# A two-layer decoder block: the shared expert's sums are copied apart and turned a unit later; the narrow attention's first head norms are formed batch by batch

## The reference

```
def _L0_ffn_ref(...):                       # 16 experts, 4 picked per row
    probs = softmax(h @ router_w.T); top_vals, top_idx = top_k(probs, 4)
    y = einsum('eni,eih->enh', silu(g) * u, w_down)
    routed = einsum('enh,ne->nh', y, comb)
    shared = silu(h @ sh_gate) * (h @ sh_up) @ sh_down     # width 704
    return routed + sigmoid(h @ sh_gate_w) * shared

def _L1_attn_ref(...):                      # 16 heads of 16 channels
    q = (_rms(x, g_q) @ Wq + bq); k, v = split(_rms(x, g_kv) @ Wkv + bkv)
    scores = einsum('bhqd,bhkd->bhqk', _rms(q, g_head), _rms(k, g_head)) * 16 ** -0.5
    return (softmax(scores) @ v) @ Wo + bo

x = x + _L0_attn_ref(_layernorm(x), ...)
x = x + _L0_xattn_ref(..., _layernorm(x), ctx)     # time mixing, a scan over the rows
x = x + _L0_ffn_ref(_layernorm(x), ...)
x = x + _L1_attn_ref(_layernorm(x), ...)
x = x + _L1_xattn_ref(_layernorm(x), ctx, ...)
x = x + _L1_ffn_ref(_layernorm(x), ...)
```

## Time and profile before

| | |
|---|---|
| median of 3 runs | 1784.8 us |
| the profiled execution | 1775.09 us, its span 1773.3 us |
| TensorE busy | 1588.2 us, 90% of the span, mean granted clock 0.957 |
| its weight loads | 1281.9 us, 72% |
| DVE / ACT / POOL busy | 1116.2 us, 63% / 946.6 us, 53% / 554.5 us, 31% |
| shared expert's group ends | transposes start at 666.1, 705.3, 740.5 and 763.5 us |
| narrow attention | first scores at 1046.4 us |

### The profile page before, as it was taken

The page is one execution under the profiler, slowest core; times in us unless marked ns, Lnnn a source line. Parts: engine busy times, 40 slices in busy tenths (PEclk is TensorE's granted clock), DMA queues, the critical chain, the costliest instruction groups (busy, mean ns, idle before and its releaser), DMA issues.

```text
span 1773.3 us, 26005 instructions
## 1 busy us (share of the span) xinstructions
PE 1588.2 (90%) x8599; PEld 1281.9 (72%) x8599; DVE 1116.2 (63%) x2497; ACT 946.6 (53%) x2996; POOL 554.5 (31%) x466
## 2 busy tenths in 40 slices
PE   6999999989998768899999769999979999999766
PEld 5888878877877556667777647777758888888534
DVE  3543675677477675454444465655467888877878
ACT  4666655556655643223323435676835565566556
POOL 2233332563254362311001554556131132211000
PEclk9999999999999988999999968989989999999988
DMA  7143234433444062133433411100031111000001
GB/s 268 31 165 127 95 121 140 153 125 105 151 156 151 30 166 66 60 103 124 129 106 115 145 46 31 43 4 25 1 140 30 33 42 34 12 1 1 1 1 48
DMA packets 85241, 147.33 MB, mean 83 GB/s; under 512 B 9700, under 2 KB 45172, under 8 KB 85108
## 3 DMA queue, kind: packets, MB, share of 16 engines
q1 hardware_dynamic: 78964, 128.89, 22.3%
q0 software_dynamic: 6144, 16.79, 3.0%
HBM read 86.65 MB, written 58.98 MB: 82 GB/s over the span
## 4 chain that ended last, share of the span: by engine, by line
PE 46%; DVE 9%; issue 3%; ACT 3%; POOL 2%; another core or an unknown queue 1%; DMA 0%; DVEq 0%; POOLq 0%; ACTq 0%
PE bank L1144 5%; PE bank L906 5%; PE bank L611 4%; PE bank L613 4%; PE bank L612 4%; PE bank L923 4%; PE bank L1135 3%; PE bank L1118 3%; PE bank L1023 2%; PE bank L1005 2%; PE bank L1107 1%; PE bank L1126 1%; PE bank L1012 1%; PE bank L897 1%; PE bank L914 1%
## 5 line engine op out<-in xcount | busy, mean ns | idle before, releaser
L2632 ACT ACTIVATE cross_attention_heads<-cross_attention_heads,small 128x128 f32<-128x128 f32 x256 | 99.6, 390 | 117.2 <-DVE small L2042 117.2
L806 PE MATMUL bank<-self_attention 128*128 128x256 f32 x512 | 125.6, 389 | 22.3 <-ACT self_attention L2376 18.9
L1144 PE MATMUL bank<-cross_attention,cross_attention_heads 128*128 128x256 f32 x512 | 122.1, 381 | 12.7 <-DVE residual L2056 8.2
L2737 POOL CAST qkv_weights_split<-self_attention 128x1024 fp32r<-128x1024 f32 x45 | 50.4, 1119 | 252.6 <-DMA self_attention<-in_wqkv 206.5
L806 PEld LDWEIGHTS bank<-self_attention 128*128 128x128 f32 x512 | 97.7, 194 | 41.2 <-issue 21.7
L2360 ACT ACTIVATE self_attention<-self_attention,small 128x128 f32<-128x128 f32 x256 | 100.2, 394 | 47.0 <-DVE small L1687 45.6
L611 PE MATMUL bank<-x_channel_major,qkv_weights_split 128*128 128x512 f32 x256 | 117.8, 460 | 6.5 <-DVE qkv_weights_split L1720 2.9
L2545 ACT ACTIVATE narrow_late<-bank,small 128x128 f32<-128x128 f32 x256 | 91.2, 376 | 51.4 <-DVE small L1913 50.9
L1144 PEld LDWEIGHTS bank<-cross_attention,cross_attention_heads 128*128 128x128 f32 x512 | 96.1, 190 | 31.2 <-DVE residual L2056 15.1
L2739 POOL TENSOR_TENSOR qkv_weights_split<-self_attention,qkv_weights_split 128x1024 fp32r<-128x1024 f32 x45 | 110.6, 2458 | 3.7
L906 PE MATMUL bank<-experts,tiles 128*128 x316 | 107.6, 463 | 0.2 <-DVE tiles L1792 0.2
(11 more groups left out here) (406 smaller groups left out, 4626.9 us busy)
## 6 DMA issues: line engine op xcount, KB each, us to landing
picked_inputs<-self_attention SPq DMA_DIRECT2D x64, 512.0 KB, 6.5
self_attention<-in_wqkv SPq DMA_DIRECT2D x48, 512.0 KB, 6.0
experts_far<-picked_inputs SPq DMA_DIRECT2D x79, 128.0 KB, 2.1
picked_outputs<-tiles SPq DMA_DIRECT2D x79, 128.0 KB, 1.7
self_attention<-in_wo SPq DMA_DIRECT2D x16, 512.0 KB
experts<-in_moe SPq DMA_DIRECT2D x4, 1408.0 KB
context_values<-context_out SPq DMA_DIRECT2D x16, 256.0 KB
cross_attention<-context_values SPq DMA_DIRECT2D x4, 1024.0 KB, 9.0
```

The costliest lines, as they stand in the source:

```text
L806: m = T.matmul(bank[7][:, 0:D], ZT_a[n % 2][:, h, :], wo_a[p % 2][:, h, :], start=h == 0, stop=h == HG - 1)
L1144: m = T.matmul(bank[7][:, 0:D], ZT_x[n % 2][:, h, :], x_wo[hg % 2][:, h, :], start=h == 0, stop=h == HG - 1)
L2632: m = S.activation(P_x[u][:, h, :], P_x[u][:, h, :], ACT.Exp, bias=negmax_x[u][:, h:h + 1], accum_out=sums_x[u][:, h:h + 1])
```

## The change

*Shared expert.* ACT copies the sums into tiles of their own, e_sum, which lie in the columns of raw4, the raw weights of the narrow attention. So that the place is free, the load of these weights (768 KB) moves in SP's program to expert tile 8. `copy_sums` stands ahead of the cast of the unit in hand, where `finish` stood behind it. TensorE turns the sums in two lots of four transposes (`turn_sum`), each behind one of the next two projections, both into bank 7; for the last group, into banks 6 and 7. DVE adds them in two lots, in the next two steps. The down projection that opens a group now waits for the copies (e_copied), and the expert tiles wait for the last adds only at their down projections.

*Narrow attention.* Logarithm, exponential and inverse root of the first group are formed batch by batch, on 32 columns each. POOL's head norm 0 comes ahead of the square of batch 3, and both gathers ahead of all squares. Only head 0 is transposed before the loop. The scores wait for one half of the spread keys where they waited for both. Two combines move between the keys, the third behind the first scores.

```diff
+HEADS = {0: 1, 1: 2, 2: 3, **{n + 13 + b: GB * g + b for g, n in FIRST_STEPS for b in range(GB)}}
+HEAD_NORMS = [0] + [GB + g for g in range(NG)]
...
-        raw4 = columns(kept, "narrow_attention_weights", KT * 3 * D).take(KT * 3 * D).rearrange("p (k c) -> p k c", k=KT)
+        raw4_all = columns(kept, "narrow_attention_weights", KT * 3 * D).take(KT * 3 * D)
+        raw4 = raw4_all.rearrange("p (k c) -> p k c", k=KT)
+        e_sum = [raw4_all[:, d * GT:(d + 1) * GT] for d in range(KT)]
...
+        def sum_bank(sums, d):
+            return bank[6 + d if sums == NG - 1 else 7]
...
                     if first:
-                        pe.wait_ge(e_added, KT * (sums - 1) + d + 1)
+                        pe.wait_ge(e_copied, KT * (sums - 1) + d + 1)
                     m = matmul3(bank[d][:, :], hi[:, d * P:(d + 1) * P], lo[:, d * P:(d + 1) * P], h_hi, h_lo, first, last)
                 m.then_inc(e_down, 1)
-                if last:
-                    for d in range(KT):
-                        pe.wait_ge(e_copied, KT * sums + d + 1)
-                        for b in range(GB):
-                            m = T.transpose(bank[d][:, b * P:(b + 1) * P], e_gate[d][:, b * P:(b + 1) * P], ident[:, :])
-                        m.then_inc(e_turned, 1)
+            def turn_sum(sums, d):
+                pe.wait_ge(e_copied, KT * sums + d + 1)
+                pe.wait_ge(a_added, NSTEP)
+                pe.wait_ge(e_added, KT * sums)
+                if sums < NG - 1:
+                    pe.wait_ge(e_added, KT * sums + d)
+                for b in range(GB):
+                    m = T.transpose(sum_bank(sums, d)[:, b * P:(b + 1) * P], e_sum[d][:, b * P:(b + 1) * P], ident[:, :])
+                m.then_inc(e_turned, 1)
...
                 if i < NUNIT:
                     up(i)
                 side.step()
+                if unturned:
+                    turn_sum(*unturned.pop(0))
                 if i >= LAG:
                     down(i - LAG)
+                    if UNITS[i - LAG][3]:
+                        unturned += [((i - LAG) // NSH, d) for d in range(KT)]
                 side.step()
             side.finish()
+            for sums, d in unturned:
+                turn_sum(sums, d)
...
                 pe.wait_ge(t_outs, n - 1)
+                pe.wait_ge(e_added, KT * NG)
                 pe.wait_ge(got_down, 16 * len(down_pieces()))
...
             pe.wait_ge(tables_set, 1)
-            pe.wait_ge(e_added, KT * NG)
...
                 pe.wait_ge(n_exp, n - 1)
-                pe.wait_ge(n_spread, bb + 1)
                 i, half = divmod(q4, 2)
+                pe.wait_ge(n_spread, 2 * bb + i + 1)
...
             for b in range(GB):
                 narrow_project(b)
-            for b in range(2):
-                narrow_heads(b)
+            narrow_heads(0)
...
+                if unadded:
+                    add_sum(*unadded.pop(0))
                 if i >= LAG and UNITS[i - LAG][3]:
-                    finish(i - LAG)
+                    unadded += [((i - LAG) // NSH, d) for d in range(KT)]
                 side.step()
             side.finish()
+            for sums, d in unadded:
+                add_sum(sums, d)
...
+            def first_inverse(b):
+                mine, sums = slice(b * 32, (b + 1) * 32), qss[:, 0, b, :]
+                dve.wait_ge(n_root, 2 * b + 2)
+                newton(sums, n_w[:, mine], sums, n_t[:, mine], DS, RMS_EPS).then_inc(n_inverse, 1)
...
+            combine(5)
             split_xt(NORM["second", 0], 1)
             keys_of(15)
+            combine(6)
             for b in range(GB):
                 narrow_project(b)
-                if b:
+                if b >= 1:
                     narrow_sums(b - 1)
+                if b >= 2:
+                    first_inverse(b - 2)
             narrow_sums(GB - 1)
-            combine(5)
-            narrow_inverse(0)
-            combine(6)
-            combine(7)
+            first_inverse(GB - 2)
+            first_inverse(GB - 1)
             for n in range(B * 4 + 6):
                 if n >= 6 and (n - 6) % 4 == 0 and n < B * 4 + 3:
                     narrow_values((n - 6) // 4)
                 if n < B * 4:
                     narrow_scores(n)
+                if n == 0:
+                    combine(7)
                 if n in COMBINE:
...
                 side.step()
-            gate_busy = [(a_scores, NSTEP)] * 2
-            def up(n):
+            def gate(n):
                 u = n % 2
                 act.wait_ge(e_up, 2 * n + 1)
-                act.wait_ge(*gate_busy[u])
+                act.wait_ge(a_scores, NSTEP)
+                act.wait_ge(e_gated, n - 1)
                 S.activation(e_gate[u], bank[2 + u][:, :], ACT.Silu).then_inc(e_silu, 1)
-                gate_busy[u] = (e_gated, n + 1)
+            def split_hidden(n):
+                u = n % 2
                 act.wait_ge(e_gated, n + 1)
                 act.wait_ge(e_down, n - 1)
                 act.wait_ge(a_output, NSTEP)
                 S.copy(e_split[u][0], e_hid[u]).then_inc(e_h_hi, 1)
-            def finish(n):
-                sums = n // NSH
+            def copy_sums(sums):
+                act.wait_ge(fill_done, 12 * NHG * NG)
                 for d in range(KT):
-                    act.wait_ge(e_down, n + 1)
-                    act.wait_ge(*gate_busy[d])
-                    S.copy(e_gate[d], bank[d][:, :]).then_inc(e_copied, 1)
-                    gate_busy[d] = (e_turned, KT * sums + d + 1)
+                    act.wait_ge(e_down, NSH * (sums + 1))
+                    act.wait_ge(e_turned, KT * (sums - 1) + d + 1)
+                    S.copy(e_sum[d], bank[d][:, :]).then_inc(e_copied, 1)
             side.finish()
             side.add(last_group())
             for i in range(NUNIT + LAG):
                 if i < NUNIT:
-                    up(i)
+                    gate(i)
+                if i >= LAG and UNITS[i - LAG][3]:
+                    copy_sums((i - LAG) // NSH)
+                if i < NUNIT:
+                    split_hidden(i)
                 if i in (1, 2):
                     split_weights(i + 3)
-                side.step()
-                if i >= LAG and UNITS[i - LAG][3]:
-                    finish(i - LAG)
-                side.step()
+                side.step(2)
...
                 act.wait_ge(t_up, n + 1)
                 act.wait_ge(t_gated, n - 1)
-                act.wait_ge(e_turned, KT * NG)
+                act.wait_ge(e_gated, NUNIT)
...
             def key_root():
                 act.wait_ge(c_squared, B)
-                act.wait_ge(n_inverse, 1)
+                act.wait_ge(n_inverse, GB)
...
+            def first_root(b):
+                w = n_w[:, b * 32:(b + 1) * 32]
+                act.wait_ge(n_summed, b + 1)
+                S.activation(w, qss[:, 0, b, :], ACT.Ln, bias=eps_rms[:, 0:1], scale=1.0 / DS).then_inc(n_root, 1)
+                act.wait_ge(n_root, 2 * b + 1)
+                S.activation(w, w, ACT.Exp, bias=log_rms[:, 0:1], scale=-0.5).then_inc(n_root, 1)
...
-            narrow_root(0)
-            for b in range(2):
-                narrow_heads(b)
+            for b in range(GB - 1):
+                first_root(b)
+            narrow_heads(0)
+            first_root(GB - 1)
...
             def head_norm(bb):
                 g, b = divmod(bb, GB)
-                pool.wait_ge(n_inverse, g + 1)
+                pool.wait_ge(n_inverse, HEAD_NORMS[g] + 1 if g else b + 1)
...
                 pool.wait_ge(n_heads, bb + 1)
                 pool.wait_ge(n_scores, 4 * (bb - 1))
                 for i in range(2):
-                    m = G.tensor_tensor(kbd[s][:, i], n_kT[bb % 8][:, i].unsqueeze(1).broadcast_to([P, HG, P]),
-                                        mask4.unsqueeze(2).broadcast_to([P, HG, P]), ALU.mult)
-                m.then_inc(n_spread, 1)
+                    G.tensor_tensor(kbd[s][:, i], n_kT[bb % 8][:, i].unsqueeze(1).broadcast_to([P, HG, P]),
+                                    mask4.unsqueeze(2).broadcast_to([P, HG, P]), ALU.mult).then_inc(n_spread, 1)
...
             inverse_deviations(NORM["second", 0], RMS_EPS * LN_EPS, 1.0 + RMS_EPS)
-            for b in range(GB):
+            gather(7)
+            gather(8)
+            for b in range(GB - 1):
                 square(b)
-            gather(7)
             head_norm(0)
-            head_norm(1)
+            square(GB - 1)
             spread_keys(0)
-            head_norm(2)
-            head_norm(3)
-            gather(8)
+            for b in range(1, GB):
+                head_norm(b)
...
                     sp.wait_ge(fill_done, 12 * NHG * NG)
-                    D_(raw4, io["wqkv1"]).then_inc(got_w4, 16)
                     fetch_value(6)
...
                 if n == 8:
+                    D_(raw4, io["wqkv1"]).then_inc(got_w4, 16)
...
```

35 lines of the change are left out of this document (17 added, 18 removed).

## The result

The kernel after takes 1770.57 us (median of 15 runs, 1763.85 to 1784.59), the kernel before 1786.64 us beside it (15 runs, 1779.33 to 1791.78). The ratio is 0.9914, with a 95% interval from 0.9899 to 0.9929: 15.4 us less, between 12.7 and 18.0. Forecast were 19.7 us less and 1765.1 us, with a range of 1758 to 1774. So the time lies in the range, and outside the 1760 to 1769 that the forecast gave for itself; the saving of 19.7 lies outside the measured interval.

What follows compares the result with a forecast made beforehand. TensorE, busy for 90% of the span, was taken as the bound, with time to gain only from its idle tenth or lower clock. Shared expert 8.7 plus narrow start 11.0 made 19.7 us: 1784.8 to 1765.1 us, range 1758 to 1774.

Steps and rivals of the forecast that it cites:

- Rival A: Shared expert gives 4 us or less, as DVE's chain and nameless delays keep it; total 15, 1770 us; chance 0.15.
- First group: Shared expert, first group's sums: DVE sets the stretch, so only 0.5 us gained, ends 0 and 1.6.
- Second: Shared expert, second group's sums: picks no longer stand behind DVE's adds; 0.8 us gained, ends -0.5 and 1.2.
- Third: Shared expert, third group's sums: 6 us gained, taken between 8.1 without the nameless delays and 3.5 to 4.2 with them.
- Its other case: Third group of the shared expert: nameless delays come again at the same instructions, leaving a gain of 3.5 to 4.2 us.
- Last: Shared expert's last group: first tile's transposes need no adds; 1.4 of 2.63 us come back, ends 0 and 2.6.
- Narrow start: Start of the narrow attention: earlier gathers, norms and scores bring score block 3 11.0 us forward, bounds 5 and 12.
- combine(7): DVE's combine behind the narrow attention's first scores, beside three norms: 2 to 4.3 us by the rows, taken as 3.
- Its signs: Shared expert and narrow start: trace marks, including tiles 6 to 11 us earlier; wrong if narrow start gives under 8.
- Rival B: Narrow start gives half: a nameless delay of 5 to 6 us beside the moved gathers; 1771 us; chance 0.14.
- Rival C: Tiles or narrow attention: later waits take back the gain; within 0.2% of 1784.8 us; chance 0.07.
- Rival D: Slower: DMA bursts delay DVE and ACT, 10 us at two points, 3 to 5 in third group; 1790; chance 0.04.

Runs made afterwards that it cites:

- undisturbed pair: The later traces of the unchanged kernels before (e9) and after (e10), without waits that have no named releaser; the two kernels took 1772.2 and 1756.0 us.
- e3: The kernel after with ACT's copies of the sums behind the cast of the unit in hand, as in the kernel before; ratio to before 0.9897.
- e11: The kernel after with ACT's copies behind the cast and POOL's inverse deviations of the narrow attention ahead of gather 6; ratio to before 0.9890.
- first pair: The first traces of the unchanged kernels before and after; the profiled execution of after took 1771.54 us, 3.6 us less than that of before.
- e1: The kernel before with the shared expert's part of the change alone; ratio to before 0.9949, 9.1 us less.
- e4: The kernel after with combines 5 and 6 back behind the first group's inverse roots; ratio to before 0.9905.
- e5: The kernel after with POOL waiting for the last group's last down projection after eight of that group's sixteen scatters; ratio to before 0.9897.
- e12: The kernel of e6 once more, unchanged; ratio to before 0.9918.
- e9: The kernel before, unchanged, timed and traced once more; ratio to before 0.999.
- e10: The kernel after, unchanged, timed and traced once more; ratio to before 0.990.
- e2: The kernel before with the narrow attention's part of the change alone; ratio to before 0.9945, 9.8 us less.
- e7: The kernel after with the gathers of batches 7 and 8 back in their old places behind the squares and head norms; ratio to before 0.9939.
- e8: The kernel after with the first group's roots formed for all four batches at once and head norms behind the fourth square; ratio to before 0.9888.
- e6: The kernel of e5 with POOL also waiting for 5, 9 and 13 keys before gathers 2, 4 and 6; ratio to before 0.9936.

## Why the prediction was right, and where not

The sum was 19.7 us; the undisturbed pair shows 17.1 and the medians 15.4. Faster was forecast, and the time is in the range, which is in part luck: the largest term of the shared expert was four times too large, two smaller ones and the narrow start were too small, and the range was wide enough for Rival A. By its steps:

*First group: forecast 0.5 less, measured 0.57 more*, in every kernel with early copies, outside the ends of 0 and 1.6. That DVE bounds it held: it has no idle time between its 5.1 us scan and 684. The step named what went against it, a colder TensorE, and gave it 1.2 us, but took the warm case as the likelier. e3 and e11 bear the clock out: the same program in this stage took 1.5 us less with the window at 1.00 than at 0.83. It doesn't hang on the place of the copies, so a first group with late copies is not safely better.

*Second: forecast 0.8, measured 1.64.* The steps came nearly as written (bank 7: 0.8 forecast, 0.47 found). The cut of 0.4 for a colder stretch was not needed.

*Third: forecast 6, measured 1.5.* This is the step that failed. It set a disturbed before, with 6.72 us idle, against an after in which the disturbance might vanish, and called 8.1 the one end. Its other case, delays on both sides, had 3.5 to 4.2, and the first pair measured 3.1. The waits without a name are no property of the kernel. They stand in all six traces taken while before ran at 1786 us (before, after, e1 to e4) and in none of the eight taken while it ran at 1771 to 1772 (e5 to e12). e1 to e4 ran on another chip than e5 to e12 (for the first pair the record names none), so the waits may belong to the chip as well as to the time; no run separates the two. The table of waits (engine, line, releaser: us, times, longest) of after and of e1:

```profile
ACT context_out L2528 <- remote: 17.3, 3, 9.6
...
DVE context_keys L1887 <- remote: 9.9, 1, 9.9
...
DVE experts L1767 <- remote: 7.2, 1, 7.2
```

```profile
ACT context_out L2517 <- remote: 16.3, 2, 9.5
DVE experts L1765 <- remote: 6.4, 1, 6.4
ACT narrow_attention_weights L2474 <- remote: 4.4, 1, 4.4
```

They lengthen 731 to 775 by 6.8 us and the keys by 12.1 us in before (against e9), by 6.8 and 12.6 in after (against e10), so they belong in neither side's account. They also change the stage behind: the projections, for which POOL then has had time, are 5.3 us shorter in before than in e9 and only 2.5 in after than in e10, which is why the row at 1017 to 1033 changes its sign between the pairs.

*Last: forecast 1.4, measured 2.5* undisturbed, near the upper end of 2.6, and 0.9 in the first pair: the first tile's transposes go ahead of the adds and DVE's copy follows these without a wait, and the rest is whether the clock falls at the tiles' start. The sum had no term for it.

*Narrow start: forecast 11.0, measured 12.2* undisturbed, 11.0 between e1 and e2, 6.8 in the first pair. Two of its numbers were off. The moved combines were charged 1.05 us; undisturbed the projections come 0.43 earlier, for there POOL's gathers, not DVE, are late beside the keys. And the pick behind combine(7), with its two moments, was put at 1.2 us, while its add alone took 2.92. Combine(7) itself took 2.53, inside the prediction's 2 to 4.3. The rule that the prediction quoted from the Trainium skill, "SBUF — State Buffer", gave up to 5 for combine(7) and a gain of 10; the combine bears out the lower price, and the time that such a rule would ask for came one instruction later, at the add. This add also makes up much of the difference between the pairs: it took 0.48 us in the first trace of before and about 3 in after, e9 and e10, so the first pair sets a lucky before against an unlucky after, by 2.5 us. What carries the gain are the early gathers (e7: 9.8 us of block 3 go with them); the roots batch by batch bring block 3 forward by 1.8 to 4.3 us and nothing that the time of e8 shows.

*Its signs.* A narrow start under 8 us was to show the prediction wrong: the first pair has 6.8, the second 12.2. The tiles were to start 6 to 11 us earlier: they start 3.5 us earlier in the first pair and 5.2 in the second. The idle time in the third group was to be 0: it is 3.32 in after and none in e10.

*Rival A* (4 us or less from the shared expert, total 15) has the total of the medians, and its mechanism by half: DVE's chain keeps the first group, but up to the tiles the change gives 5.1 us in the first pair and 5.0 in the second, and e1's time 9.1. *Rival B's* wait without a name beside the moved gathers did come in the first trace of after, 3.75 us on ACT before 1025.62; what it cost isn't shown, and undisturbed there is none. *Rival C's* fear, that what is won is taken back behind, came true in single executions only. *Rival D* (slower) did not come. Between 1060 and 1260 us, where nothing was changed, the windows of e10 and e8 read:

```profile
1060.00:1260.00 200.00, 187.81 (x1134) 149.92 (x1132) 110.40 (x229) 132.63 (x552) 94.16 (x96) 0.88 0.06 19
```

```profile
1060.00:1260.00 200.00, 187.82 (x1179) 150.83 (x1180) 113.61 (x234) 137.23 (x568) 94.66 (x96) 0.92 0.06 19
```

The same busy time holds 45 matmuls more in e8, at a granted clock of 0.92 against 0.88; from score block 3 to 1265 us of before e10 takes 8.9 us more. What moves the clock here isn't shown, and a shift in time alone does not: e9 and e10 enter this stretch 17.1 us apart and take the same time over it to 0.01 us. The 8.9 us are enough to hide the 1 to 2 us by which e3, e4, e8 and e11 could differ from after. None of them is shown to beat it, and the 4.4 us that the first pair loses behind 1059 us lie in this stretch too.

## What to carry to other kernels

An idle time is a term of the sum only if the kernel makes it: one whose releaser has no name, on an engine with its inputs ready, should stand on both sides of the account until a second trace of the same kernel has it. Work moved out from in front of an engine that waits helps as far as the next waiting place of the same chain: here 9.70 us of waiting became 3.48 and 6.25. And the early issue of a gather was worth more than the shorter chain behind it.

## What was not expected of the hardware

In six traces ACT and DVE stood for up to 12.3 us (ACT in e3) with inputs ready while POOL issued 16 or 20 indirect DMAs in a row, and ACT up to 3.9 us beside the eight moved gathers; in the others they never did, with the same rows of DMAs. What it depends on, the chip or the time, wasn't found, and whether spacing the DMAs helps then wasn't tested, since both tries (e6, e12) fell where the waits were absent. The first add of batch 8 took 0.48 us in the first trace of before and 3.02 in the second. DVE and then POOL in the second, e9_before:

```profile
1043.11 3.02 DVE L1766 SCALAR_TENSOR_TENSOR residual<-narrow_later,dispatch,residual 128x256 f32<-128x256 f32 x1 [6.22 <-DMA narrow_later<-picked_outputs,dispatch]
```

```profile
1043.80 2.05 POOL L2910 TENSOR_TENSOR narrow_late<-narrow_attention,small 128x512 f32<-128x512 f32 x2
```

The add is recorded until 1046.13, just past the end of POOL's two spreads at 1045.85. In the first trace it ran at 1055.35, POOL's pair began at 1056.08, and it took 0.48. So the add started 0.69 us ahead of POOL's pair in the one and 0.73 in the other: 0.04 us of difference, and 2.5 us in the time of block 3, more than several edits of this change. Of the 14 traces nine have the long add (2.92 to 3.02 us), started 0.58 to 0.69 us ahead of POOL's pair; five have the short one (before, e3, e4, e5, e8), started 0.73 to 1.32 us ahead, but 0.38 in e4. By the Trainium skill ("SBUF — State Buffer", who interferes with whom) the two engines exclude each other for whole instructions. The ends of the long adds, 0.3 us behind POOL's pair, agree; their starts don't show it, since an add of 0.48 us would have been over before the recorded start of the pair, and no run here took the POOL work away. Last, e6 and e12, one kernel on two chips, agree stage by stage to 0.04 us up to the last projections, while before and e9, one kernel too, part by 7.8 us between score block 3 and 1265 us.
